# A two-lane, 32-item decoder kernel: the next item's recurrence started inside its predecessor, centring folded into weights, K and V formed ahead

## The reference

```python
x = _layernorm(x + L0_attn(x));  x = _layernorm(x + L0_xattn(x, ctx));  x = _layernorm(x + L0_ffn(x))
x = _layernorm(x + L1_attn(x));  x = _layernorm(x + L1_xattn(x, ctx));  x = _layernorm(x + L1_ffn(x))

def L0_attn(x):
    x = x + min_gru(rmsnorm(x, w_mix))        # g, d, v projections, sigmoid, tanh, scan over 128 tokens
    x = x + sliding_attn(rmsnorm(x, w_attn))  # 16 heads of 8, causal
    return x + glu_ffn(rmsnorm(x, w_ffn))     # 128 -> 512 -> 128
```

## Time and profile before

| | us |
|---|---|
| median of three runs (2874.41 to 2887.03) | 2877.29 |
| profiled execution, its own time | 2874.83 |
| its span, first to last instruction | 2873.0 |
| TensorE busy | 2519.8 (88%) |
| VectorE busy | 1665.5 (58%) |
| ScalarE busy | 1636.1 (57%) |
| GpSimd busy | 306.3 (11%) |

### The profile page before, as it was taken

How to read it: one execution, slowest core, us unless ns; L and a number is a source line. 1 busy time by engine, 2 the same in 40 slices (tenths; PEclk the granted TensorE clock), 3 DMA queues, 4 the chain that set the end, 5 groups by cost and what they waited for, 6 DMA issues and landing times.

```text
span 2873.0 us, 93842 instructions
## 1 busy us (share of the span) xinstructions
PE 2519.8 (88%) x41608; PEld 1839.7 (64%) x41608; DVE 1665.5 (58%) x3917; ACT 1636.1 (57%) x3841; POOL 306.3 (11%) x270
## 2 busy tenths in 40 slices
PE   3888888888888883999999999999999999999997
PEld 1665565555665661677777777776776776777775
DVE  3556665566556655455655556566565565566564
ACT  2655565556655660565665665565565565565663
POOL 0000000000000000111111111111111111111111
PEclk9999999999999995999999999999999999999998
DMA  3000000000000001000000000000000000000000
GB/s 101 6 6 8 6 6 9 7 6 6 6 7 7 6 5 50 5 7 8 6 7 8 6 7 8 6 7 8 7 7 8 7 6 8 7 7 8 7 6 4
DMA packets 50652, 29.18 MB, mean 10 GB/s; under 512 B 19792, under 2 KB 48528, under 8 KB 50256
## 3 DMA queue, kind: packets, MB, share of 16 engines
q1 hardware_dynamic: 50256, 23.25, 2.9%
HBM read 17.98 MB, written 5.24 MB: 8 GB/s over the span
## 4 chain that ended last, share of the span: by engine, by line
PE 24%; issue 18%; DVE 10%; ACT 6%; POOL 2%; DMA 0%; POOLq 0%; SPq 0%
DVE zels L443 3%; DVE m L441 2%; PE bank L353 2%; PE bank L1217 2%; ACT zels L1335 1%; POOL PT L995 1%; PE bank L1201 1%; PE bank L1306 1%; PE bank L371 1%; ACT PT L1335 1%; PE bank L1117 1%; PE bank L1154 1%; PE bank L1203 1%; PE bank L1312 1%; PE bank L388 1%
## 5 line engine op out<-in xcount | busy, mean ns | idle before, releaser
L353 PE MATMUL bank<-w_gate,ident 128*128 128x256 f32 (+3 forms) x1664 | 487.1, 379 | 0.1
L995 POOL TENSOR_TENSOR PT<-zels,unit 128x512 f32<-128x512 f32 x160 | 203.8, 1274 | 1057.7 <-ACT zels L1335 894.2
L419 ACT ACTIVATE zels<-zels 128x512 f32<-128x512 f32 x384 | 235.3, 625 | 114.9 <-DVE zels L443 110.1
L441 DVE TENSOR_REDUCE m<-bank 128x4 f32<-128x512 f32 x384 | 262.1, 682 | 50.5 <-PE bank L378 24.1
L353 PEld LDWEIGHTS bank<-w_gate,ident 128*128 128x128 f32 x1664 | 258.3, 192 | 37.4 <-issue 23.1
L443 DVE TENSOR_TENSOR zels<-bank,m 128x512 f32<-128x512 f32 x384 | 265.5, 692 | 13.3
L388 PE MATMUL bank<-ident,zels 128*128 128x128 f32 x1536 | 229.5, 281 | 26.8 <-ACT zels L419 24.3
L458 POOL TENSOR_TENSOR Kbd<-kT,headmask 128x512 f32<-128x512 f32 x96 | 100.5, 1047 | 1417.4 <-DVE kT L436 1417.4
L422 ACT ACTIVATE PT<-bank 128x512 f32<-128x512 f32 x384 | 206.0, 593 | 16.2 <-PE bank L388 16.2
L388 PEld LDWEIGHTS bank<-ident,zels 128*128 128x128 f32 x1536 | 172.6, 142 | 61.9 <-ACT zels L419 42.0
L1335 ACT ACTIVATE zels<-bank 128x512 f32<-128x512 f32 (+1 forms) x256 | 141.9, 570 | 92.3 <-PE bank L1186 55.6
(11 more groups left out here) (283 smaller groups left out, 5129.2 us busy)
## 6 DMA issues: line engine op xcount, KB each, us to landing
ctxT<-in_ctxT_dram SPq DMA_DIRECT2D x64, 48.0 KB, 1.8
x<-in_xT_dram SPq DMA_DIRECT2D x32, 64.0 KB
x_after_cross_attention<-x SPq DMA_DIRECT2D x32, 64.0 KB, 1.6
h<-x_after_cross_attention SPq DMA_DIRECT2D x8, 256.0 KB, 2.8
xin<-x_after_cross_attention SPq DMA_DIRECT2D x32, 64.0 KB, 1.9
out_dram<-xn SPq DMA_DIRECT2D x32, 64.0 KB, 1.6
input_integers<-xq SPq DMA_DIRECT2D x8, 128.0 KB, 2.0
xq<-input_integers SPq DMA_DIRECT2D x32, 32.0 KB, 1.9
```

Of the source, the lines that this page charges most:

```text
L353: mm(bank[:, 0:cols], ident[:, :], w_gate[:, :, :].rearrange("p a b -> p (a b)")[:, 0:cols], start=True, stop=True)
L419: act.activation(n.zels[:, u, :], n.zels[:, u, :], ACT.Exp, scale=ATT_SCALE).then_inc(ph.act[s], ph.AC.step(s, f"{t}P{u}"))
L441: dve.tensor_reduce(top, scores, AX_X, ALU.max).then_inc(ph.dve[s], ph.DV.step(s, f"{t}max{u}"))
L995: pool.tensor_tensor(n.TI[:, k % 2, :, :], (n.PT0, n.PT1)[k % 2][:, :, 1, :], unit[:, :].unsqueeze(1).broadcast_to([P, NP, DK]), ALU.add)\
```

## The change

1. **The front in its predecessor.** The front's steps get semaphores of their own (`pg`) and buffers that the first stage didn't use. The stage list is rotated: a round begins with `ln1` to `ln2v` of the item before, with `load`, `rms1`, `gdv`, `gdvS`, `rms2` of the item itself placed between them, and goes on with self attention and feed-forward part. The front's results go to bank 3 of the lane. The wait for the predecessor's last VectorE step moves to `skv`. The load of x0 is issued by ScalarE in `ffn`.
2. **Centring folded in.** During set-up TensorE multiplies `w_out`, `w_xo` and `w_o1` by `center`, and ScalarE copies the results. `down`, `xWo` and `Wo1` add `center` times the residual into the same PSUM bank, so that the adds L824, L834 and L1584 and the separate stages `ln1`, `ln2`, `lng` on TensorE go; L826 moves to `rms3`, and L1584 becomes an add of the bias in `norm1`.
3. **K and V ahead.** `qkv` becomes `kv` and `q`. The context's K and V (`xkv`, `ykv`) are formed before the item reaches its cross attention.
4. **K spread by VectorE**, straight from PSUM; the copy `kT` and GpSimd's L458 go.
5. **New order strings and filler counts**: 21 units for an item of the first stage, 13 for one of the last.

```diff
+                act.wait_ge(ph.pe[s], ph.PE.upto(it, t + "kv"))
+                if t != "s":
+                    act.wait_ge(ph.dve[s], ph.DV.upto(it, t + "Kbd"))
...
+                dve.tensor_tensor(n.Kbd[:, 0:HU, :], b[KEYS[t]][:, 0:P].unsqueeze(1).broadcast_to([P, HU, P]),
+                                  headmask[:, :].unsqueeze(2).broadcast_to([P, HU, P]), ALU.mult).then_inc(ph.dve[s], ph.DV.step(s, t + "Kbd"))
...
-            pool.wait_ge(ph.dve[s], ph.DV.upto(it, t + "k"))
-            pool.wait_ge(ph.pe[s], readers_done)
-            pool.tensor_tensor(n.Kbd[:, 0:HU, :], n.kT[:, :].unsqueeze(1).broadcast_to([P, HU, P]),
...
+        XTAILS = ("ln1", "ln1v", *["x" + x for x in ATTENTION_STAGES], "xWo", "ln2", "ln2v")
+        FRONT = {"ln1": ("load",), "ln1v": ("rms1",), "xPV": ("gdv",), "xAT": ("gdvS",), "ln2v": ("rms2",)}
+        STAGES = (*[x for tail in XTAILS for x in (tail, *FRONT.get(tail, ()))],
+                  "skv", *["s" + x for x in ATTENTION_STAGES], "sWo", "rms3", "xkv", "ffn", "down")
...
-        WARM = {"rms1": 0, "gdv": 0, "rms2": 7, "sqkv": 3, "sWo": 0, "rms3": 1, "ffn": 0, "down": 1, "ln1": 2,
-                "ln1v": 1, "xqkv": 3, "xWo": 3, "ln2": 2, "ln2v": 1, "s": {"S": 1, "P": 0, "OT": 4, "AT": 1},
-                "x": {"S": 1, "P": 0, "OT": 1, "AT": 1}}
+        WARM = {"rms1": 2, "gdv": 0, "rms2": 0, "skv": 1, "sWo": 0, "rms3": 4, "ffn": 0, "down": 0, "ln1v": 0,
+                "xq": 4, "xWo": 0, "ln2v": 0, "s": {"S": 3, "P": 0, "OT": 2, "AT": 0},
+                "x": {"S": 1, "P": 0, "OT": 4, "AT": 0}}
...
                     if stage == "rms1":
+                        if it > 0:
+                            pe.wait_ge(dve_did[s], DV.upto(it - 1, "hidden"))
+                        keep_warm(b[3], WARM["rms1"])
+                        pe.wait_ge(pg.act[s], pg.AC.upto(it, "sq1"))
+                        mm(b[3][:, 0:P], mean[:, :], n.sqf[:, :], start=True, stop=True).then_inc(pg.pe[s], pg.PE.step(s, "rms1"))
...
+                            if stage == "skv":
+                                pe.wait_ge(dve_did[s], DV.before(it))
+                                keep_warm(b[1], WARM["skv"])
+                                pe.wait_ge(pg.dve[s], pg.DV.upto(it, "xn2"))
...
+                        pe.wait_ge(dve_did[s], DV.upto(it, "xr"))
+                        mm(b[0][:, 0:P], center[:, :], n.x3[:, :], start=True, stop=False)
                         pe.wait_ge(dve_did[s], DV.upto(it, "hidden"))
...
+                        mm(b[1][:, 0:P], center[:, :], n.x1[:, :], start=True, stop=False)
                         pe.wait_ge(act_did[s], AC.upto(it, "xAT"))
+                        mm(b[1][:, 0:P], w_xo[:, :], n.AOT[:, :], start=False, stop=True).then_inc(pe_did[s], PE.step(s, "xWo"))
...
+                        if it + 1 < ROUNDS:
+                            act.wait_ge(dve_did[s], DV.upto(it, "xr"))
+                            act.dma_start(n.x0[:, :], a["xT"][(it + 1) * LANES + s]).then_inc(pg.loaded[s], 16)
...
+                            if p == 3:
+                                mm(b[2][:, 0:P], center[:, :], n.x3[:, :], start=False, stop=False)
...
-        CWARM = {"h": 0, "conv": 2, "alpha": 0, "F": 0, "norm1": 0, "bc": 0, "fc": 1, "pj": 2, "yqkv": 2, "Wo1": 0,
-                 "lna": 0, "lnav": 1, "lng": 0, "lngv": 2, "lny": 1, "lnyv": 0, "lnf": 2, "lnfv": 0,
-                 "y": {"S": 0, "P": 0, "OT": 2, "AT": 0}}
+        CWARM = {"h": 0, "conv": 2, "alpha": 3, "F": 0, "norm1": 0, "bc": 0, "fc": 4, "pj": 0, "yq": 1, "Wo1": 0,
+                 "lna": 1, "lnav": 0, "lngv": 1, "lny": 0, "lnyv": 0, "lnf": 0, "lnfv": 1,
+                 "y": {"S": 0, "P": 0, "OT": 0, "AT": 0}}
```

More of the change, by code:

```diff
@@ L145, in in_rounds @@
                 advance(s, it - back, stage)
-ATTENTION_STAGES = ("qkv", "Kbd", *[f"S{u}" for u in range(NU)], *[f"P{u}" for u in range(NU)], "PV", "OT", "norm", "AT")
+ATTENTION_STAGES = ("q", *[f"S{u}" for u in range(NU)], *[f"P{u}" for u in range(NU)], "PV", "OT", "norm", "AT")
 def decoder(nc, a):
@@ new lines, in decoder @@
+        s_pe, s_act, s_dve = attention_steps("s")
+        x_pe, x_act, x_dve = attention_steps("x")
+        pg = Part(sem, "g",
+            ["rms1", "gdv", "rms2"],
+            ["sq1", "rms1l", "rms1", "gdE", "vE", "gdvL", "gdvS", "sq2", "rms2l", "rms2"],
+            ["xn1", "zg", "zd", "zv", "th", "a", "xs", "scan", "x1", "xn2"],
+            ["none"])
+        ph = Part(sem, "a",
+            [*s_pe, "sWo", "rms3", x_pe[0], "gate", "up", "down", "ln1v", *x_pe[1:], "xWo", "ln2v"],
+            [*s_act, "sAT", "sq3", "rms3l", "rms3", x_act[0], "gateE", "gateL", "gateS", "ln1sq", "ln1l", "ln1r", *x_act[1:], "xAT", "ln2sq", "ln2l", "ln2r"],
+            [*s_dve, "x2", "xr", "xn3", x_dve[0], "zgate", "silu", "hidden", "ln1", "mask", *x_dve[1:], "ln2", "top", "mx"],
+            ["none"])
@@ L542, in _ @@
             def _(pe):
+                pe.wait_ge(turned_loaded, 16 * 3)
                 pe.wait_ge(weights_loaded, 16 * (len(LOADS) + 3))
+                banks = lane[1].bank
+                for j in range(FT):
+                    last = mm(banks[0][:, j * P:(j + 1) * P], w_out_t[:, j * P:(j + 1) * P], center[:, :], start=True, stop=True)
+                last.then_inc(w_centred, 1)
+                mm(banks[1][:, 0:P], w_xo_t, center[:, :], start=True, stop=True).then_inc(w_centred, 1)
+                for p in range(NP):
+                    last = mm(banks[2 + p // 4][:, p % 4 * P:(p % 4 + 1) * P], w_o1_t[:, p * P:(p + 1) * P], center[:, :], start=True, stop=True)
+                last.then_inc(w_centred, 1)
                 pe.wait_ge(w_ready, W_QUANTISED)
@@ L662, in advance @@
                         for j in range(3):
-                            last = mm(b[1][:, j * P:(j + 1) * P], w_gdv[:, j, :], n.xn[:, :], start=True, stop=True)
-                        last.then_inc(pe_did[s], PE.step(s, "gdv"))
+                            last = mm(b[3][:, (j + 1) * P:(j + 2) * P], w_gdv[:, j, :], n.xnf[:, :], start=True, stop=True)
+                        last.then_inc(pg.pe[s], pg.PE.step(s, "gdv"))
                     if stage == "rms2":
-                        keep_warm(b[0], WARM["rms2"])
```

372 lines of the change are left out of this document (175 added, 197 removed).

## The result

The changed kernel takes 2697.5 us (median of 4 runs, 2695.9 to 2701.5), the kernel before 2878.7: ratio 0.937, 95% interval 0.934 to 0.939. I had said 2693. That the total came so close is luck: the first stage gave 18 us more than I said and the last one 23 us less, and the step behind the first stage's number was wrong.

A forecast was written before the change was run, and what follows sets the result against it. The lane's chain was taken to bound the first stage, TensorE plus a small wait after the change. 2874.8 less 141 (first stage), 42 (last stage) and 1 (set-up) gave 2691, at the median's level 2693 us; range 2640 to 2745 (0.60).

The forecast's parts named there:

- Front, 9.2 us: First stage: the front moved beside the predecessor's cross-attention tail leaves the lane's chain, 9.2 us a round.
- That is less than TensorE needs: First stage: the 50.1 us chain lies below TensorE's busy 51.6; with 3.4 us idle the round is 55.0 us.
- bare chain of 50.1 us: First stage: one lane's round after the gains, 64.4 - 9.2 - 0.9 - 1.9 - 1.2 - 1.1 us.
- The small terms, 0.9 + 1.9 + 2.3: First stage, us off a round's chain: K spread by VectorE 0.9, context K and V ahead 1.9, centring folded 2.3.
- Fillers: First stage: 12 fewer filler units for each of two items cut TensorE's busy time by 5.2 us a round.
- First stage in all: First stage with set-up: 142 us gained, mainly from rounds falling from 64.4 to 55.0 us.
- Last stage: -2.6 us a round said: Last stage: centring folded (0.8) and K and V ahead (1.8) shorten each round by 2.6 us, -42 us in all.
- wrong if less than 1: Last stage: the forecast is wrong if its round moves by less than 1 or more than 5 us.
- the round is 106.0 - 2.6: Last stage: the chain's 2.6 us come off the round in full, giving 103.4 us with TensorE idle for 5.9.
- Wide: Rival, both stages: front formed late, waits stay as they are; 59.2 and 105.1 us a round, 2788 us; chance 0.17.
- The clock: Rival, either stage: fewer fillers drop the granted clock to 0.61; 3030 us if for a fifth of it; chance 0.04.

## Why the prediction was right, and where it was not

**Front, 9.2 us.** The mechanism is as foreseen in the trace: xn within a microsecond of the predecessor's last step, GpSimd empty. The size, 9.5 with the order, is near, but it is more than the whole stage gained at equal fillers (8.2, below), so it confirms no term of a sum.

**"That is less than TensorE needs": this step failed.** I had a bare chain of 50.1 us, found TensorE's 51.6 above it and added 3.4 of idle time to get 55.0. The round came out at 54.0, near 55.0 for a wrong reason: with no filler at all and the clock at 1.00 it is 54.0 too. TensorE's time doesn't set it; a chain of waits does, 3.9 us longer than my bare steps. That these are stands behind the other lane's work is what the run with K and V late suggests; they weren't taken apart. The 51.6 was off as well. TensorE is busy 49.3 us, and with the same 33 units as before 53.1 (742.86 / 14) against 56.8, so its busy time did not fall only by the fillers.

**The small terms, 0.9 + 1.9 + 2.3.** I took each as the length of its own instructions and added them to the overlap. Undone one at a time at equal fillers and full clock, they and the overlap are worth 5.2, 3.5 and 9.5, together 18.2, while the whole first stage gained 64.4 - 56.2 = 8.2 at 33 units. With the overlap gone and the old order back, having the other three brings nothing (65.7 against 64.4). They aren't terms of a sum. Each was undone in an order and with filler counts fitted to the whole, so its price holds the misfit too; a new fit after each undoing, which might lower the prices, was not made. K's spread alone was not undone, only doubled.

**Fillers.** I took 24 units as 5.2 us less of TensorE's time and so of the round. From 33 to 21 gave 2.2 us, from 21 to none 0 at the same clock, in the old order 0.1.

**First stage in all:** 142 us said, 160.1 measured; 14 rounds of 10.4 gave 145.9 (901.8 - 755.9), the end of the stage 14.8 (73.4 and 58.5 us from the fifteenth store to the middle part), its beginning -0.6.

**Last stage: -2.6 us a round said, -1.0 measured**, just inside the bound that said "wrong if less than 1". In quiet rounds it is 1.65, of which four filler units are 0.7. TensorE's idle time is 7.1 us in the quiet round above and 7.7 in the mean, where I had 5.9; before it was 7.6. The step that failed is "the round is 106.0 - 2.6": the bare steps of an item that runs alone were taken off the round in full. In the old order the same edits take nothing off it (105.5). *Wide*, for this stage, was the better picture: TensorE waits as long as before, and its 105.1 was nearly the 105.0 measured. What sets a quiet round there isn't settled: four units more cost 0.7 us, eight fewer gave 0.1 or 0.7, and a run at full clock without fillers, as in the first stage, was not to be had.

**The clock.** In the first stage it stayed at 1.00, as I had it. The rule of the Trainium skill (TensorE: Matmul & The Clock Gate, on HAM oscillation), that idle gaps bring the lower level back, agrees with the run without fillers: 0.94 and 0.96, and 70 us more than the changed kernel. I gave it 0.04 for this change; three of the variants whose round is longer at the same 21 units show 0.92 to 0.95, so the lower level was nearer than I thought.

## What to carry to other kernels

A busy time plus a guessed idle share gives a round's length only by luck; take the filler work away and find a round at full clock: if it is as long as before, the engine's own time isn't what sets it. Where two lanes share in-order engines, the price of a step is what stands in front of it in each queue: undo steps one at a time in the new order and try them once in the old, and don't add the results. A fitted order and its filler counts go together, and have to be measured again, with the granted clock beside each time, after every edit.

## What the runs showed of the hardware that I had not expected

The clock falls in short pieces inside a stage whose mean is 1.00. The round of 107.7 us begins in such a piece. First four windows of the changed kernel (two ahead of it, its beginning, its middle):

```profile
1390.00:1395.00 5.00, 4.66 (x228) 4.30 (x218) 4.43 (x12) 1.39 (x3) 0.00 (x0) 1.00 0.02 3
1395.00:1397.00 2.00, 0.48 (x9) 0.38 (x11) 0.67 (x2) 0.00 (x0) 0.00 (x0) 1.00 0.00 0
1397.00:1399.00 2.00, 2.00 (x37) 1.61 (x40) 0.00 (x0) 1.51 (x3) 0.00 (x0) 0.65 0.04 8
...
1401.00:1408.00 7.00, 6.76 (x39) 6.54 (x40) 2.56 (x6) 1.12 (x4) 0.00 (x0) 0.51 0.03 9
```

then TensorE's timeline there, and in the last two lines the same instructions in the quiet round:

```profile
1395.58 0.35 PE L1277 MATMUL bank<-Qz,S 64*64 64x64 f32 x5 [0.80 <-DVE S L1592]
1396.87 0.79 PE L1277 MATMUL bank<-Qz,S 64*64 64x64 f32 x20 [0.94 <-issue]
...
1401.24 2.08 PE L1294 MATMUL bank<-f,expand 64*128 64x128 f32 x16 [0.27 <-DVE f L1598]
...
1405.11 1.91 PE L1301 MATMUL bank<-zels,w_o 128*128 128x128 f32 x8
...
1717.36 1.16 PE L1294 MATMUL bank<-f,expand 64*128 64x128 f32 x16 [0.42 <-DVE f L1598]
...
1719.45 1.06 PE L1301 MATMUL bank<-zels,w_o 128*128 128x128 f32 x8
```

From 1401 to 1408 the granted clock is 0.51, the lower level of 1.2 GHz, and matmuls take 1.8 times as long. What came before it: TensorE was busy for 4.66 of 5 us, then for 0.48 of 2, because an issue wait of 0.94 us came right behind the ordinary one of 0.80 for S. In the quiet round TensorE waits 0.65 us for S at the same place (1713.44) and no issue wait follows. So the two disturbances may be one at times, an issue wait at a place that is thin already, and then the clock; this is one such piece read from a trace, not a run that shows the cause.

The issue waits, up to 1.6 us each in the changed kernel, go with the order: 5.8 to 9.8 us over 14 rounds of the last stage in the three kernels with its old order, 15 to 22 in all the others, whatever the fillers. Most of them come at packs of small matmuls (10.9 of 18.4 us at L1218 to L1238, 32 of 64x64 in 0.69 us).

The traces say more about what they are. The page of the changed kernel lists a DMA queue that carries instructions:

```profile
q8 instruction: 323, 5.29, 0.8%
```

In the last stage one of its packets of 16 KB lands every 6.2 us on average. The wait of 1.61 us above ends at 2287.51, 1.35 us after a packet landed (2284.93 to 2286.16), the one of 0.94 at 1396.87, 1.34 us after another (1394.15 to 1395.53). So it is with all 19 issue waits over 0.33 us in that stage of the changed kernel: each ends 1.2 to 1.65 us after a landing, a stretch in which a wait without any tie to the packets would end in one case of 14. The five of the kernel before and the three of the last stage in the old order do the same. **So these waits look like waits for instructions that have not arrived**; the tie is in the times, and no run changed the loading. Short waits at L1262, 0.3 us in many rounds, don't follow the packets and are something else. That the two orders differ in how closely the packs of small matmuls, which use up instructions fastest, follow on each other is my guess at why the order matters; no run took it apart.
